# Six local layers as one loop of 192 groups, the feed-forward spread over attention steps

## The reference

```python
for i in range(DEPTH):                                   # 6
    x = attn_layer(shift_tokens(x), Wqkv[i], q_scale[i], k_scale[i], Wo[i]) + x
    x = ffn_layer(shift_tokens(x), ln_g[i], ln_b[i], W1[i], b1[i], W2[i], b2[i]) + x
```

## Time and profile before

| | |
|---|---|
| median of 3 runs | 3058.05 us (3054.85 to 3058.92) |
| the profiled execution | 3054.89 us, span 3053.1 us |
| PE busy | 2715.1 us, 89% of the span |
| DVE, ACT, POOL busy | 2102.4, 1914.1, 1582.0 us |
| granted clock of PE, mean | 0.942 |

### The profile page before, as it was taken

The page is one execution under the profiler, slowest core; times in us unless marked ns, Lnnn a source line. Parts: engine busy times, 40 slices in busy tenths (PEclk is TensorE's granted clock), DMA queues, the critical chain, the costliest instruction groups (busy, mean ns, idle before and its releaser), DMA issues. The chain is left out here.

```text
span 3053.1 us, 69434 instructions
## 1 busy us (share of the span) xinstructions
PE 2715.1 (89%) x27218; PEld 1734.3 (57%) x27218; DVE 2102.4 (69%) x4064; ACT 1914.1 (63%) x5192; POOL 1582.0 (52%) x1845
## 2 busy tenths in 40 slices
PE   5996999899989998899889988999789977986995
PEld 2553777477746775577557764777334434542552
DVE  3764898598948994899679866897455434745663
ACT  3444888488848885788668875887323343554343
POOL 0523887288818882788468854887043003300530
PEclk8898999999999999999999999999989997998797
DMA  2001000100010001000100010000100000000000
GB/s 99 2 2 45 19 17 18 42 18 19 18 41 17 19 17 36 23 19 17 39 21 17 19 41 17 19 17 16 36 1 2 1 0 1 2 1 0 2 2 14
DMA packets 35934, 57.89 MB, mean 19 GB/s; under 512 B 7200, under 2 KB 32800, under 8 KB 33952
## 3 DMA queue, kind: packets, MB, share of 16 engines
q1 hardware_dynamic: 35616, 53.52, 5.6%
HBM read 27.28 MB, written 1.05 MB: 9 GB/s over the span
## 5 line engine op out<-in xcount | busy, mean ns | idle before, releaser
L1052 POOL TENSOR_TENSOR l_qk<-l_ta,l_tb 128x256 f32<-128x256 f32 x768 | 540.1, 738 | 113.9 <-DVE l_tb L1106 113.7
L674 POOL TENSOR_SCALAR qmr<-q_all,cf 128x256 fp32r<-128x256 f32 x128 | 116.2, 927 | 711.9 <-SPq L475 378.1
L1068 POOL TENSOR_TENSOR l_qk<-l_qk,l_rn 128x512 f32<-128x512 f32 x384 | 392.8, 1044 | 133.5 <-DVE l_rn L1131 133.5
L706 DVE TENSOR_REDUCE mrow<-ring 128x2 f32<-128x512 f32 x512 | 324.4, 684 | 197.7 <-PE ring L522 185.4
L1059 POOL TENSOR_TENSOR l_pr<-l_pr,l_rs 128x512 f32<-128x512 f32 x384 | 392.7, 1047 | 42.5 <-DVE l_rs L1121 42.5
L973 ACT ACTIVATE l_pr<-st,l_mn 128x128 f32<-128x128 f32 x1152 | 355.0, 384 | 85.9 <-DVE l_mn L1094 85.9
L659 ACT ACTIVATE pt<-st 128x512 f32<-128x512 f32 x384 | 200.2, 600 | 289.2 <-PE st L557 289.2
L1110 DVE TENSOR_REDUCE l_n<-l_sq 128x8 f32<-128x512 f32 x384 | 250.1, 660 | 27.6 <-ACT l_sq L982 26.8
L547 PE MATMUL st<-qm,k_all 32*128 32x512 f32 x1024 | 223.0, 672 | 0.0
L835 PE MATMUL ring<-l_wa,l_xs 128*128 128x512 f32 x384 | 195.0, 631 | 27.5 <-DMA l_wa<-in_wa 13.0
L522 PE MATMUL ring<-ktr,qmr 32*128 32x256 f32 x1024 | 198.5, 396 | 14.4 <-POOL qmr L674 11.9
(11 more groups left out here) (238 smaller groups left out, 6365.9 us busy)
## 6 DMA issues: line engine op xcount, KB each, us to landing
l_vm<-l_v SPq DMA_DIRECT2D x192, 96.0 KB, 2.0
l_wa<-in_wa SPq DMA_DIRECT2D x7, 2048.0 KB, 9.4
l_vm<-l_v SPq DMA_DIRECT2D x192, 32.0 KB, 1.9
l_wf<-in_wf SPq DMA_DIRECT2D x6, 580.5 KB, 3.7
w<-in_w SPq DMA_DIRECT2D x1, 2752.0 KB, 15.6
cf<-in_cf SPq DMA_DIRECT2D x1, 1123.0 KB, 17.7
x<-in_xT SPq DMA_DIRECT2D x1, 1024.0 KB, 4.8
ctxT<-in_ctxT SPq DMA_DIRECT2D x1, 1024.0 KB, 8.1
```

Of the source, the lines that this page charges most:

```text
L706: dve.tensor_reduce(mrow[b % 2][:, t, j, 2 * p:2 * p + 2], bank_of(f"R{r}").rearrange("p (h k) -> p h k", h=2), AX.X, ALU.max).then_inc(ri ...
L1052: ins = pool.tensor_tensor(halves[0][:, :, x], halves[1][:, :, x], halves[2][:, :, 1 - x], ALU.add)
L1068: pool.tensor_tensor(part, part, t.rn[:, :, 4 * x:4 * x + 4].unsqueeze(3).broadcast_to([P, 2, 4, LHD]), ALU.mult).then_inc(qk_normed, 1)
```

## The change

`local_attention` and `local_ffn` become one function, `local_layers`, with one block. The loop runs over 192 groups of all layers, and PE, ACT, POOL and DVE run their steps for N from -2 to 199. The attention part of a step keeps its order on each engine. `chunk_at(N, lag)` says whether step N does a part of a chunk's feed-forward: chunk q has its parts in steps 8q+7+lag. Every part stands at the end of a step on ACT, POOL and DVE, and on PE ahead of `rows`:

- lag 3, DVE: copy with shift into `fs`
- lag 4: centering on PE, copy on ACT into `fc`, square on POOL
- lag 5: mean on PE, logarithm and exponential on ACT, product on POOL
- lag 6, DVE: scale and bias
- lag 7: three pairs on PE, Gelus on ACT (the table loads stand ahead of the V copy and behind the last Gelu), gates on DVE
- lag 8: the products back on PE, update on DVE

The square, and the product with the inverse root, move from ACT and DVE to POOL. The feed-forward uses attention's PSUM banks (`ffn_bank`, `pair_banks`) with added waits. `wa` and the tables `tab` have two buffers; SP issues the next layer's weights between gathers at group 6, and `wf` at group 11. The shift for a batch of the next layer waits for the update of its chunk. The feed-forward has memory of its own. The load of a seventh layer's weights is gone.

```diff
...
+BATCHES = DEPTH * NB
+STEPS = GROUPS * BATCHES
+LAYER = GROUPS * NB
 GQ = INNER // GROUPS
...
-def local_attention(g, d, t):
+def local_layers(g, t):
...
+    def chunk_at(N, lag):
+        q, at = divmod(N - 2 * GROUPS + 1 - lag, 2 * GROUPS)
+        return q if at == 0 and 0 <= q < BATCHES // 2 else None
+    def ffn_bank(N):
+        return bank(g, "T1", N)
...
+    def pair_banks(N, i):
+        if i == 0:
+            return bank(g, "R0", N + 1), bank(g, "R1", N + 1)
+        if i == 1:
+            return bank(g, "P0", N + 3), bank(g, "P1", N + 3)
+        return bank(g, "T0", N), bank(g, "T1", N)
...
+            sp.dma_start(t.wf[:, :], g.a["wf"][:, cols(0, D_ALL - D_W1)]).then_inc(wf_loaded, 16)
+            for N in range(STEPS):
+                d, k = divmod(N, LAYER)
...
                 sp.wait_ge(ring_act, 3 * N + 3)
                 sp.dma_start(t.vm[0:RSPAN, at], t.v[0:RSPAN, 1, at]).then_inc(values_gathered, 16)
                 sp.dma_start(t.vm[RSPAN:P, at], t.v[RSPAN:P, 0, at]).then_inc(values_gathered, 16)
+                if k == 6 and d + 1 < DEPTH:
+                    if d:
+                        sp.wait_ge(out_filled, LAYER * d)
+                    sp.wait_ge(tables, 4 * d + 4)
+                    load_attention_weights(g, d + 1, t, sp)
+                if k == 11 and d:
+                    sp.wait_ge(updated, 4 * d)
+                    sp.dma_start(t.wf[:, :], g.a["wf"][:, cols(d, D_ALL - D_W1)]).then_inc(wf_loaded, 16)
...
-            def project(s, N, k, j):
-                if j == 1 and k >= 1:
+            def project(N, j):
+                d, k = N // LAYER, N % GROUPS
+                wa = t.wa[d % 2]
...
+                if j == 1 and N >= 1:
                     pe.wait_ge(ring_act, 3 * N)
...
             def turn_probs(N, k):
                 pe.wait_ge(p_normed, 2 * N + 2)
+                if chunk_at(N, 7) is not None:
+                    pe.wait_ge(gated, FFC * chunk_at(N, 7) + 3)
                 for tile in range(2):
+                    if tile == 1:
+                        ffn_bank_read(N)
                     for x in range(4):
                         c, hh = divmod(x, 2)
                         mm = pe.transpose(bank(g, f"T{tile}", k)[:, x * P:(x + 1) * P],
                                           t.pr[:, k % 2, hh, c, tile, :], g.f("ident"))
                     mm.then_inc(p_turned, 1)
+            def ffn_bank_read(N):
+                if chunk_at(N, 4) is not None:
+                    pe.wait_ge(center_copied, chunk_at(N, 4) + 1)
+                if chunk_at(N, 5) is not None:
+                    pe.wait_ge(rstd, 2 * chunk_at(N, 5) + 1)
+                if chunk_at(N, 8) is not None:
+                    pe.wait_ge(updated, chunk_at(N, 8) + 1)
...
+            def center(N, q):
+                pe.wait_ge(f_shifted, q + 1)
+                pe.matmul(ffn_bank(N), g.f("center"), t.fs[:, :], start=True, stop=True).then_inc(centered, 1)
+            def mean_square(N, q):
+                pe.wait_ge(squared, q + 1)
+                pe.matmul(ffn_bank(N), g.f("mean"), t.fsq[:, :], start=True, stop=True).then_inc(variance, 1)
+            def pairs(N, q):
+                pe.wait_ge(normed, q + 1)
+                for i in range(FFC):
+                    if i == 1 and N + AHEAD < STEPS:
+                        pe.wait_ge(ring_act, 3 * (N + AHEAD) + 3)
+                    for x in range(2):
+                        mm = pe.matmul(pair_banks(N, i)[x], t.wf[:, (x * FFC + i) * P:(x * FFC + i + 1) * P], t.xn[:, :],
+                                       start=True, stop=True)
+                    mm.then_inc(pair_filled, 1)
+            def down(N, q):
+                pe.wait_ge(gated, FFC * q + FFC)
+                for i in range(FFC):
+                    w2 = D_W2 - D_W1 + i * P
+                    mm = pe.matmul(ffn_bank(N), t.wf[:, w2:w2 + P], t.h[:, i, :], start=i == 0, stop=i == FFC - 1)
+                mm.then_inc(sum_filled, 1)
+            def feed_forward(N):
+                for lag, work in ((4, center), (5, mean_square), (7, pairs), (8, down)):
+                    if chunk_at(N, lag) is not None:
+                        work(N, chunk_at(N, lag))
+            def step(N):
+                if N + AHEAD < STEPS:
+                    project(N + AHEAD, 0)
+                    project(N + AHEAD, 1)
+                if 1 <= N <= STEPS:
+                    turn_probs(N - 1, N - 1)
+                if N >= 2 and N + AHEAD < STEPS:
+                    project(N + AHEAD, 2)
+                if 2 <= N < STEPS + 2:
+                    project_back(N - 2)
+                if 0 <= N + 1 < STEPS:
+                    turn(N + 1, N + 1)
+                if 2 <= N <= STEPS:
+                    sum_values(N - 1, N - 1)
+                if -1 <= N < 1:
+                    wait_for_rows(N, N)
+                if N < 2:
+                    project(N + AHEAD, 2)
+                if N == 1:
+                    sum_values(N - 1, N - 1)
+                feed_forward(N)
+                if 0 <= N + 1 < STEPS:
+                    if chunk_at(N, 7) is not None:
+                        pe.wait_ge(gated, FFC * chunk_at(N, 7) + 1)
+                    rows(N + 1, N + 1)
+            for N in range(-AHEAD, STEPS + 2 * GROUPS):
+                step(N)
...
+            def copy_centered(N, q):
+                act.wait_ge(centered, q + 1)
+                act.activation(t.fc[:, :], ffn_bank(N), ACT.Copy).then_inc(center_copied, 1)
+            def inverse_root(N, q):
+                act.wait_ge(variance, q + 1)
+                act.activation(t.frs[:, :], ffn_bank(N), ACT.Ln, bias=g.f("eps5", 1)).then_inc(rstd, 1)
+                act.wait_ge(rstd, 2 * q + 1)
+                act.activation(t.frs[:, :], t.frs[:, :], ACT.Exp, scale=-0.5).then_inc(rstd, 1)
+            def gelus(N, q):
+                for i in range(FFC):
+                    act.wait_ge(pair_filled, FFC * q + i + 1)
+                    act.activation(t.gl[:, i, :], pair_banks(N, i)[1], ACT.Gelu,
+                                   bias=t.wf[:, vec + 2 + FFC + i:vec + 3 + FFC + i]).then_inc(gelu_done, 1)
+                act.preload_act_table_set(EXP_AND_LN)
...
+            def feed_forward(N):
+                for lag, work in ((4, copy_centered), (5, inverse_root), (7, gelus)):
+                    if chunk_at(N, lag) is not None:
+                        work(N, chunk_at(N, lag))
...
+                    inverse_norms(N + AHEAD)
+                if chunk_at(N, 7) is not None:
+                    act.preload_act_table_set(GELU)
+                if N + AHEAD < STEPS:
+                    values_to_sbuf(N + AHEAD, N + AHEAD)
+                if 1 <= N <= STEPS:
+                    sums_to_sbuf(N - 1, N - 1)
+                feed_forward(N)
+            for N in range(-AHEAD, STEPS + 2 * GROUPS):
...
+            def make_tables(d):
+                pool.wait_ge(w_loaded, d * 32 + 32)
+                for i, name in enumerate(("lqcos", "lqsin", "lkcos", "lksin")):
...
+            def feed_forward(N):
+                q = chunk_at(N, 4)
+                if q is not None:
+                    pool.wait_ge(center_copied, q + 1)
+                    pool.tensor_tensor(t.fsq[:, :], t.fc[:, :], t.fc[:, :], ALU.mult).then_inc(squared, 1)
+                q = chunk_at(N, 5)
+                if q is not None:
+                    pool.wait_ge(rstd, 2 * q + 2)
+                    pool.tensor_tensor(t.xn[:, :], t.fc[:, :], t.frs[:, :], ALU.mult).then_inc(scaled, 1)
...
+                feed_forward(N)
+                if N % LAYER == 14 and N // LAYER + 1 < DEPTH:
+                    make_tables(N // LAYER + 1)
+            make_tables(0)
+            for N in range(-AHEAD, STEPS + 2 * GROUPS):
+                step(N)
...
-            def shift(b):
+            def shift(s):
+                b = s % NB
+                if s >= NB:
+                    dve.wait_ge(updated, 4 * (s // NB - 1) + b // 2 + 1)
...
+            def shift_chunk(N, q):
+                dve.wait_ge(y_added, 2 * q + 2)
+                src = g.y[:, cols(q % 4)].rearrange("p (b s) -> p b s", b=2)
+                dst = t.fs[:, :].rearrange("p (b s) -> p b s", b=2)
+                dve.tensor_copy(dst[0:64], src[0:64])
+                dve.tensor_copy(dst[64:P, :, 1:SEQ], src[64:P, :, 0:SEQ - 1]).then_inc(f_shifted, 1)
+            def gain_and_bias(N, q):
+                dve.wait_ge(wf_loaded, 16 * (q // 4) + 16)
+                dve.wait_ge(scaled, q + 1)
+                dve.tensor_scalar(t.xn[:, :], t.xn[:, :], gain, bias, ALU.mult, ALU.add).then_inc(normed, 1)
+            def gates(N, q):
+                for i in range(FFC):
+                    dve.wait_ge(gelu_done, FFC * q + i + 1)
+                    dve.scalar_tensor_tensor(out=t.h[:, i, :], in0=pair_banks(N, i)[0],
+                                             scalar=t.wf[:, vec + 2 + i:vec + 3 + i], in1=t.gl[:, i, :],
```

(59 more changed lines are left out.)

263 lines of the change are left out of this document (59 added, 204 removed).

## The result

After: 3030.15 us, the median of 6 runs (3026.91 to 3036.76); before, timed along with it, 3056.67 (3054.41 to 3059.99). The ratio is 0.9914 with an interval of 0.9901 to 0.9926: 26.5 us or 0.9% faster, where 41.7 us had been forecast. The profiled execution took 3027.85 us, its span 3026.1. The six local layers shrank from 1922.75 us to 1896.05 (start of the first shift copy at 64x255, 259.75 and 257.27 us, to the end of the last update, 2182.50 and 2153.32), 26.7 of the 27.0 us by which the two spans differ. So the rest of the kernel has no part in the result, and the question is what a chunk cost.

What follows compares the result with a forecast made beforehand. Bound: a 7.87 us ring over PE, ACT and DVE, plus 61.5 us per layer beside steady steps. Removed 350.5, added 23 x 12.6 + 22 - 3 = 308.8: 41.7 saved from 3058.05, 3016.4 us; own range 2998 to 3037, full 2972 to 3056.

Steps and rivals of the forecast that it cites:

- Removed: Five layer boundaries with drain and refill, feed-forward included, at 61.5 us each, plus 42.97 us for the last layer: 350.5 us.
- PE work of a chunk: Eleven products of 128x512 between value sums and score rows on PE, 0.86 us each: 9.44 us, paid in full.
- Pairs: Lag 7: second pair waits for the V copy behind the Gelu table load; step costs 6.04 us, 0.88 over PE work.
- Center, mean, down: Lags 4, 5, 8: the added work on ACT, DVE and POOL is hidden; each costs 0.5 us if that cover goes.
- DVE alone: Lags 3 and 6: two shift copies, 1.73 us with one POOL wait, less 0.1 of air; scale and bias 0.55 us.
- Queues: SP's weight loads between gathers, the next layer's small tables and shift waits: all nought, some 12 us of margin left.
- Tail: Last chunk, with no attention to hide in: 22 us; the chunk before it partly hides in the drain: -3.
- Rival A: The ring absorbs more of the copies, scale and pairs step: 10.8 us a chunk, 83 saved, 2975 us; chance 17%.
- the ring: One steady attention step across PE, ACT and DVE, 7.87 us with almost no air; PE has 0.37 us of slack.
- Rival B: POOL wins the port before each shift copy and the scale: 14.8 us a chunk, 9 slower, 3067 us; chance 13%.
- Rival C: Each ACT table switch costs twice its 1.28 us load: 15.2 us a chunk, 18 slower, 3076 us; chance 5%.
- Rival D: Granted clock falls to 0.97 under a denser PE, or queues change phase: 3045 us; chance 10%.

Runs made afterwards that it cites:

- three small moves: Against the changed kernel: Gelu table load put behind the V copy, scale and bias moved to ACT, upper shift copy moved to ACT; 2966.9 us.

## Why the prediction was right, and where it was off

Direction and mechanism held, and 3030 lies in the forecast's own range (2998 to 3037); the gain was 26.5 and not 41.7 us.

- *Removed, 350.5:* right within 1%. The run without a feed-forward gives 353.0.
- *PE work of a chunk, 11 x 0.86:* **this is the term that was mis-sized.** It priced products by their rate among their like the earlier trace rows, although each batch of them now stands between tiles of another shape, and the earlier trace rows names those tiles. Four insertions at 0.2 us are 0.8 us a chunk, 23 x 0.8 = 18 us, where the whole miss is 15.0; the pairs step has 0.1 more a chunk, and 0.09 too much in each of the two steps of DVE alone (4 us) and the 2.5 us of the boundaries went the other way.
- *Pairs, 0.88 over PE's work:* mechanism right, 1.18 measured. The forecast read the steps of one kind and applied them to another. This step adds an output, the one in the earlier trace rows does not. In such a step the exponential of the norms starts 0.68 after the last value part, not 0.35 (623.59 to 623.94), and it did so in before already. PE's and ACT's timelines of before:

```profile
655.56 0.45 PE L916 MATMUL ov<-l_pt,l_vm 128*64 128x64 f32 x8 [0.36 <-ACT l_kt L992]
...
656.25 0.31 ACT L1005 ACTIVATE l_rn<-l_lnv,cf 128x16 f32<-128x16 f32 x1
```

  That is why the V copy came 0.35 later than worked out. Counted from the last value part, the exponentials of the next step start at 8.8 and not at 8.3, and without a chunk at 2.45 in such a step and not at 2.26, so the 0.5 us missed there are 0.3 in the price of the chunk. Of the 0.5, 0.35 are the V copy; the insertion's 0.10 going in is hidden in that wait, but PE pays 0.10 once more behind it, and 0.09 coming out. What holds the exponential of the norms appears to be POOL: the small operation on DVE ahead of it (L1240, 0.72 us here, 0.43 in a plain step) ends 0.03 to 0.04 us behind an instruction of POOL's in 191 of the 192 groups (mostly its first product of L1168), and took 0.17 in the one that is left. That it waits there for a port they share is how these ends are read; no run moved POOL away from it. That the table load stood in the way was in the sum; that its move behind the V copy gives 0.87 back a chunk was not seen.
- *Center, mean, down:* what ACT, DVE and POOL do for them was hidden, as said: center costs exactly what its product costs, and doubled, exactly one product more.
- *DVE alone:* 1.64 and 0.46 for 1.73 and 0.55. The order of the two copies and POOL's products was as forecast, copy (0.41), then wait and copy (1.17). The 0.1 us of air subtracted there did not exist: the starts of the two copies and of what follows them lie 0.43 and 1.20 apart, 1.63 of the 1.64. The Trainium skill (SBUF — State Buffer, "Who interferes with whom") says that whoever issues first holds the ports for its whole instruction. The rows agree instruction by instruction; but the prediction's reading of it, that the result must be either end, was wrong, as with two instructions on each side they alternate.
- *Queues:* right: nothing waits for SP, shifts or gathers. But "the small tables go into a step of the pairs" at nought is right by its cover alone; without it they cost 0.74 to 1.76 us a layer.
- *Tail:* 21.85 for 22. The -3 for the chunk before it comes out near, too: 326.3 less 23 x 13.34 leaves 19.5 for the last chunk net, where 19 was forecast. That 22 came so close is partly luck: it adds up a dozen rounded terms, and no row had the wait of 0.15 for a semaphore.
- *Rival A* fell: nothing was absorbed, as the ring had no air. *Rival B* fell in its strong form: POOL wins one product per chunk, not three. *Rival C* fell: after the load of 1.28 us at 1103.63 the next activation starts at 1104.92, 0.01 later. The Trainium skill (ScalarE: Activation LUTs, "What ACT_TABLE_LOAD costs") adds a drain of 1.38 us; with the load in the middle of the stream this trace shows none. *Rival D* fell: the granted clock is 1.00 over a thousand microseconds.

## What to carry to other kernels

Work that is spread into a tight ring costs what it adds to the engine that holds the ring at that point, in the neighbourhood in which it lands: price a product at a change of tile shape, a copy beside GpSimd, a table load by what stands behind it, and not by the row from a stage where each ran among its like. Once the period of the ring is constant, the excess of each step over its twin without the extra work is a bill with one line for each edit, and lines can then be moved one at a time to the engine that is idle at that point; here three small moves took 2.67 us of 13.3 off each chunk, 62 us in all and more than the whole change had won. And a step is priced by the rows of a step of its own kind: those with an addition of an output ran 0.35 us later at one point than the plain one that had been read. An engine's idle time in one step is a budget to be read first: ACT had room for one copy of 0.62 us and not for two.

## What the runs showed of the hardware that was not expected

- A float32 product of 128*128 between products of 128*64 and of 64*64 costs 0.10 us on going in and 0.09 on coming out; with 64 columns it costs 0.37 us in all. The 0.10 also falls on a product behind a wait of PE with no change of shape (1105.57), the 0.09 also between turns of 128*128 and value sums of 128*64, all float32.
- Where DVE and GpSimd both have two instructions to issue, they alternate: 0.41, then 1.17 for a copy of the same size, and 2.34 for POOL's two in place of 2.05.
- A copy of 64x512 from SBUF to SBUF took 0.62 us on ACT and 0.41 on DVE, and a scale and bias of 128x512 0.81 and 0.54; ACT's were still the cheaper ones where they were off the ring.
- An operation of DVE on 128x16 elements (L1240) took 0.42 to 0.74 us and ended 0.03 to 0.04 us behind an instruction of POOL's in 191 of 192 groups; in the other it took 0.17.
- A table load between two activations took 1.28 us and no more, with its neighbours on the engine 0.02 and 0.01 us away.
